# Loops of six edge tiles instead of five, and the zeroing of two DRAM buffers and a broadcast load moved behind the blocks of 32 destinations

## The reference

```python
xn = _layernorm(x)
x = x + gnn(xn @ W, edges) + linear_attention(xn)    # gnn: relu(sum over edges of edge_weight * (xn @ W)[src])
x = x + moe_block(_layernorm(x))                     # attention, gate, one of 8 experts per node
xn = _layernorm(x)
x = x + graph_attention_2_layers(xn, edges) + linear_attention_2(xn)
x = x + ffn_top2(_layernorm(x))
```

## Time and profile before

| | us |
|---|---|
| median of 3 runs | 1269.78 (1269.62 to 1273.46) |
| the profiled execution's own time | 1271.01 |
| its span | 1269.5 |
| PE busy | 1103.7 (87%) |
| DVE busy | 540.2 (43%) |
| ACT busy | 356.5 (28%) |
| POOL busy | 105.8 (8%) |

### The profile page before, as it was taken

How to read it: one execution, slowest core, us unless ns; L and a number is a source line. 1 busy time by engine, 2 the same in 40 slices (tenths; PEclk the granted TensorE clock), 3 DMA queues, 4 the chain that set the end, 5 groups by cost and what they waited for, 6 DMA issues and landing times.

```text
span 1269.5 us, 20489 instructions
## 1 busy us (share of the span) xinstructions
PE 1103.7 (87%) x7358; PEld 747.2 (59%) x7359; DVE 540.2 (43%) x1451; ACT 356.5 (28%) x901; POOL 105.8 (8%) x170
## 2 busy tenths in 40 slices
PE   4477899889999837999998579998979998997898
PEld 2367754647777433555554257786557777573763
DVE  7577773344446411111111145543325545368350
ACT  1001230014555221222222135443115555011230
POOL 5112300000000050000000230000000000000000
PEclk9799999989999957999999889999989999998799
DMA  7500014100000258910499470000121000000001
GB/s 219 130 1 2 2 64 169 58 1 25 26 26 2 83 209 298 396 48 17 178 405 400 176 278 26 26 1 1 67 74 43 26 10 2 34 1 1 1 8 33
DMA packets 19105, 113.09 MB, mean 89 GB/s; under 512 B 4906, under 2 KB 6433, under 8 KB 14948
## 3 DMA queue, kind: packets, MB, share of 16 engines
q1 hardware_dynamic: 13406, 100.95, 21.1%
q0 software_dynamic: 5632, 11.23, 3.3%
HBM read 103.04 MB, written 9.11 MB: 88 GB/s over the span
## 4 chain that ended last, share of the span: by engine, by line
PE 75%; DVE 10%; DMA 6%; issue 4%; ACT 3%; DVEq 1%; POOL 1%; SPq 0%; POOLq 0%; ACTq 0%
PE psum L543 10%; PE psum L694 9%; PE psum L844 7%; PE psum L825 7%; PE psum L717 5%; PE psum L555 5%; PE psum L748 5%; PE psum L699 5%; PE psum L604 4%; PE psum L730 4%; PE psum L903 3%; PE psum L925 3%; DMA arena<-in_moe_b 2%; DVE arena L1214 2%; PE psum L782 1%
## 5 line engine op out<-in xcount | busy, mean ns | idle before, releaser
L543 PE MATMUL psum<-arena 128*125 128x512 f32 x320 | 142.7, 606 | 1.8 <-ACT arena L938 1.4
L998 ACT ACTIVATE arena<-arena,small 125x625 f32<-125x625 f32 x120 | 97.0, 809 | 90.5 <-DVE small L1340 90.5
L694 PE MATMUL psum<-arena 128*128 128x313 f32 (+1 forms) x384 | 112.5, 444 | 8.4 <-DMA arena<-in_att 7.1
L543 PEld LDWEIGHTS psum<-arena 128*125 128x125 f32 x320 | 61.0, 192 | 80.4 <-issue 75.3
L825 PE MATMUL psum<-arena 128*64 128x512 f32 x448 | 100.2, 600 | 6.5 <-DMA arena<-in_moeW 5.1
L844 PE MATMUL psum<-arena 128*64 128x256 f32 x896 | 99.8, 381 | 3.5 <-DMA arena<-in_moe_b 3.5
L1056 ACT ACTIVATE arena<-psum,cols 128x64 f32<-128x64 f32 x224 | 47.3, 361 | 195.9 <-PE psum L831 195.9
L694 PEld LDWEIGHTS psum<-arena 128*128 128x128 f32 x384 | 72.4, 195 | 38.0 <-issue 9.7
L604 PE MATMUL psum<-arena 125*128 x1150 | 74.2, 223 | 23.1 <-DVE arena L1214 23.1
L1214 DVE TENSOR_SCALAR arena<-arena 125x628 bf16<-125x628 f16 x230 | 77.0, 399 | 35.3 <-PE psum L604 20.3
L1340 DVE CUSTOM_DVE_ANT_0 arena<-psum,cnt_adj 125x625 f32<-125x625 f32 x80 | 61.5, 806 | 71.6 <-PE psum L717 71.6
(11 more groups left out here) (246 smaller groups left out, 1321.8 us busy)
## 6 DMA issues: line engine op xcount, KB each, us to landing
arena<-in_moeW SPq DMA_DIRECT2D x16, 4096.0 KB, 17.9
arena<-in_att SPq DMA_DIRECT2D x36, 256.0 KB, 2.8
arena<-in_l1W SPq DMA_DIRECT2D x2, 2048.0 KB, 15.8
token_rows<-arena POOLq DMA_DIRECT2D x19, 128.0 KB, 13.1
rows<-in_rows SPq DMA_DIRECT2D x1, 2240.0 KB
expert_rows<-arena POOLq DMA_DIRECT2D x17, 128.0 KB, 13.0
arena<-token_rows POOLq DMA_DIRECT2D x16, 128.0 KB, 7.8
arena<-in_gnnWo SPq DMA_DIRECT2D x2, 1024.0 KB, 6.1
```

Source lines behind the costliest of these rows:

```text
L543: mm = pe.matmul(bank(b, NP, D), srcT[:, k, c * NP:(c + 1) * NP], ring[n % 2][:, k, :], start=(k == 0), stop=(k == KC - 1))
L694: mm = pe.matmul(bank(b, P, width), aw[:, w, k, :], srcT[:, k, o:o + width], start=(k == 0), stop=(k == KC - 1))
L998: act.activation(Sx[u % 3][h], Sx[u % 3][h], ACT.Exp, bias=small[0:NP, 80 + n:81 + n], scale=-1.0, accum_out=small[0:NP, 120 + n:121 + n]) ...
```

## The change

`GT` is 6: six tiles a turn, six buffers, and one more padded tile (`TP` 165 instead of 164). The turns of the 20 windows, counted on the inputs, go from 8, 4, 3, 3, 2, 2, 2, 2, 2, 2, 2, 2, 2, 2, 2, 1, 2, 1, 1, 1 (46 turns, 230 tiles) to 7, 3, 3, 2, 2, 2, 2, 2, 2, 2, 1, 1, 1, 1, 1, 1, 1, 1, 1, 1 (37 turns, 222 tiles).

SP sends `rows` only when all windows are done. POOL zeroes the DRAM buffers after the last window's sums. The zeroed piece of SBUF that this reads lies elsewhere, so ACT waits for the zeroing before it writes there (T3, in stage moT).

```diff
-GT = 5
+GT = 6
...
-        zero_rows_sb = at(o_D + TP * 2 * DW, TT, D)
+        zero_rows_sb = at(o_T + 2 * KC * N + 2 * NC * 3 * DW, TT, D)
...
             sp.dma_start(cols[:], ins["cols"]).then_inc(ld_const, 16)
-            for p in SPLIT:
-                sp.dma_start(rows[p], ins["rows"].partition_broadcast(p.stop - p.start)).then_inc(ld_const, 16)
             sp.dma_start(gate_b[:], ins["gate_b"].partition_broadcast(NP)).then_inc(ld_const, 16)
...
+            sp.wait_ge(win_full, NW)
+            for p in SPLIT:
+                sp.dma_start(rows[p], ins["rows"].partition_broadcast(p.stop - p.start)).then_inc(ld_const, 16)
...
-            pool.wait_ge(ld_ring[0], 16)
-            pool.wait_ge(consts, 14)
-            for t in range(MAXT + 2):
-
-                pool.dma_start(xs_dram[t * TT:(t + 1) * TT, :], zero_rows_sb).then_inc(
-                    zero_rows if t <= MAXT else M["st"], 16)
-                if t < MAXT:
-                    pool.dma_start(ys_dram[t * TT:(t + 1) * TT, :], zero_rows_sb).then_inc(zero_rows, 16)
...
             pool.memset(bd[:, :, :], 0.0).then_inc(bd_zero, 1)
+            pool.wait_ge(consts, 14)
+            for t in range(MAXT + 2):
+
+                pool.dma_start(xs_dram[t * TT:(t + 1) * TT, :], zero_rows_sb).then_inc(
+                    zero_rows if t <= MAXT else M["st"], 16)
+                if t < MAXT:
+                    pool.dma_start(ys_dram[t * TT:(t + 1) * TT, :], zero_rows_sb).then_inc(zero_rows, 16)
...
             feature_exps(range(8, 8 + NC))
+            act.wait_ge(zero_rows, 16 * (2 * MAXT + 1))
+            act.wait_ge(M["st"], 16)
             cols_out("moT", T3)
```

More of the change, by code:

```diff
@@ L189, in build @@
         parts = [at(o_T + 2 * KC * N + i * NC * 3 * DW, NP, NC, 3 * DW) for i in range(2)]
-        assert o_D + TP * 2 * DW + D <= AR
         assert oa[0] <= o_cnt
```

## The result

The changed kernel takes 1255.2 us (median of 4 runs, 1252.92 to 1260.38) against 1270.38 us for the kernel before (4 runs, 1269.62 to 1273.46) on the same chip: ratio 0.9875, 95% interval 0.9848 to 0.9901. The nearest case was the rival "loads freed", 1257.2. The profiled execution is the longest of the four: span 1258.8, own time 1260.38, where before it was 1269.5 and 1271.0. So the two traces hold 10.7 us of the 15.2 us between the medians. The other 4.5 lie between runs of one and the same kernel, and no trace shows them.

What follows compares the result with a forecast made beforehand. The prediction took PE, busy for 87% of the span, as the bound. Turns -7.8, padding +0.1, loads 0, constants +5.6 and clock +1.0 gave -1.1 us from the median 1269.8: 1268.7 us, range 1256 to 1273.

Steps and rivals of the forecast that it cites:

- loads freed: Rival: DMA traffic slowed the register loads, so the windows start 11.5 us earlier; 1257.2 us, chance 0.35.
- Part 1: Window loops: nine turns fewer save 19.3 us, the added tiles cost up to 11.5; gain 7.8 us taken, bounds 7.8 to 11.2.
- the sixth tile: Tile added to each of the 37 turns: 0.31 us each on PE, 11.5 us in all, or down to 0.22, 8.1 us.
- free tiles: Rival: the window loops' added tile hides in PE's idle time, 37 x 0.22; 1265.3 us, lower edge of the forecast's 0.52.
- Part 2: Register loads ahead of the windows: DMA silence leaves them long, gain 0; bounds no gain to 11.5 us earlier.
- Part 3: Row constants sent at the windows' end (W) land at W + 10.8, making mq's last unit 5.6 us late; bounds 4.3 and 9.8.
- the landing beyond W + 13: Sign against the forecast: mq's first unit coming later than 13 us after the windows' end (W).
- the start before 54: Sign against the forecast: PE's first window matmul before 54 us, meaning the register loads felt the traffic.
- windows under 88: Sign against the forecast: windows shorter than 88 us, meaning the added tile hides.
- Part 4: PE's clock may fall while it idles ahead of agg, ending agg later: 1.0 us taken, bounds 0 and 1.8.
- Part 5: Late zeroing, done 30 to 34 us after the windows' end, stays hidden by 0 to 4 us behind the mask; no cost.
- The sum: Whole kernel: turns -7.8, padding +0.1, loads 0, constants +5.6, clock +1.0, together -1.1 us.

Runs made afterwards that it cites:

- turns_alone: Changed kernel with both transfers (row constants and zeroing) back in their early places, loops of six kept: 1247.94 us, ratio 0.9823.
- turns_unaligned: Six tiles a turn, both transfers early, and the loaded numbers two words further on, at word 4998, off a multiple of four: 1260.29 us, ratio 0.9919.
- loads_by_place: Separate kernel computing nothing of the reference: PE loads 20 registers from many SBUF places, quiet, beside zeroing, beside weight loads; 1.36 to 4.93 us a load when quiet.
- five_late: Changed kernel with five tiles a turn instead of six, so `bounds` at word 4678, both transfers late: 1268.94 us, ratio 1.0008.
- aligned_alone: Kernel before with two words left empty, so `bounds` starts at word 4680, a multiple of four, instead of 4678: 1257.37 us, ratio 0.9903.
- rows_early: Changed kernel with the row constants sent early again, zeroing still late: 1247.1 us, ratio 0.9823.
- changed_again: Changed kernel, no edit, measured and profiled once more: 1254.29 us, ratio 0.9874.
- zero_early: Changed kernel with the zeroing back in its early place, row constants still late: 1259.56 us, ratio 0.9901.
- zeroed_piece_moved: Kernel before with only the SBUF piece that the zeroing reads (and ACT's wait) moved to its place in the changed kernel: 1267.46 us, ratio 0.9975.
- rows_after_first_window: Changed kernel with the row constants sent when the first window, not the last, has filled: 1246.06 us, ratio 0.9794.

## Why the prediction was wrong

**Part 1, turns: right in kind, too small.** 37 turns came, and the windows took 87.8 us where 90.6 were predicted: -10.4, inside the bounds of 7.8 to 11.2. The mis-sized term is the sixth tile. I charged PE's 0.31 us. From the two lengths, the 37 added tiles cost 19.3 - 10.4 = 8.9 us, 0.24 each. That is close to my rival "free tiles" (0.22), but not for its reason: the sixth tile doesn't hide in PE's idle time, for the wait on DVE ahead of a turn is 0.50 us in both kernels (23.1 us in 46 turns, 18.4 in 37). A turn's matmuls run 1.57 us for five tiles and 1.83 to 1.85 for six in the timelines, so one tile more costs PE itself 0.26 to 0.28; 0.31 was the mean of five, with what the group costs once in it. The windows are as long in turns_alone and turns_unaligned, with all transfers early.

**Part 2, the start: the step that failed.** "I take the long loads as they are: gain 0." The gain was 11.9 us (13.3 like with like). I had argued from the loads of one register, 298 to 327 ns even in a stretch of 545 GB/s, that traffic doesn't slow a load. That was the wrong witness, twice. The 545 GB/s are a mean over 2 us: from 693.5 to 694.5, around the load at 693.9, the trace has no packet at all. And the traffic of that stretch is weights coming in from DRAM, which slows no load (4.76, 1.36 and 0.30 us beside it in loads_by_place, the last of them amid packets); what ran at the start was the zeroing, out of SBUF, and that does. A share of busy DMA engines doesn't say what kind of transfer it is.

The second half was in neither my forecast nor my rival: the price of a bulk load depends on where its first number lies, 1.4 or 4.8 us quiet, 5.6 or 18.9 beside the zeroing. The diff moves `bounds` by 318 words without naming it. So the rival "loads freed" came near in time, with half the reason: its bound was 46.0 for the first window matmul, by 0.30 us a register; the loads then took 0.08 a register, and PE's stage ahead, which ended at 43.44, set the start at 45.67. Its mechanism was real: traffic slowed the loads, and quiet alone gave 9.7 to 11.0 us of the start (five_late). But it wasn't needed: the place alone gave 10.7 (aligned_alone), and with the place right the late zeroing brings the start from 46.03 to 44.24 and no time that could be told (turns_alone and rows_early, both 0.9823). The two gains overlap; they don't add. That the whole came out at the rival's 1257.2 is luck in part: a larger gain at the start and in the windows met a larger loss behind them.

The Trainium skill's rule of about 200 ns a register ("Runtime: NRT & Kernel Launch", section "Instruction fetch mechanics"), which I had set against the trace, agrees with one of the four cases here: 20 unaligned registers, quiet, 4.74 to 4.93 us, 0.24 each. Aligned they cost 0.07. The Trainium skill has that section's load and store prices for registers that the runtime loads; here the numbers lie in SBUF, and the measurement decides. The rule gave the right doubt, that something slowed the load. The start of 44.2 that I had worked out by it, held by `hot_dst`, is where changed_again and rows_early have it (44.24), but with a load of 1.55 us and not of 4: DVE's builder sets it.

**Part 3, the constants: the right mechanism, +7.9 for +5.6.** The eight units took 13.3 us (146.88 to 160.16), as worked out (13.4). The mis-sized term is the landing, W + 13.4 for W + 10.8. I had taken 323 GB/s from the queue's rate with other loads, 7.9 us, and 1.5 us besides; with the engines for itself (zero_early) this broadcast had its packets in 10 us and released DVE 3 us after the last. My reason for the long end of the bounds, the zeroing beside it, was wrong: there was none in zero_early. With the landing beyond W + 13, a sign that I had named as "wrong" came, as did two others, the start before 54 and windows under 88; and by my own sum, -1.1 + 2.6 = +1.5, the kernel would have been no faster, had the rest come as forecast. five_late, without the turns, shows how a quiet start and this loss cancel.

**Part 4, the clock: +2.1 for +1.0,** a little over its upper bound of 1.8. It fell before agg, as feared: 0.50 from 154.1 to 167.7, and agg 23.90 us against 21.69 where it didn't fall. The transposes in between, on which I had counted, did not keep it up: from the end of mq's matmuls, 150.56, to 154.1 they were 0.99 us of work. All four traces with late constants have the half clock at agg's start (agg 23.20 to 23.95 us); of the nine with early ones eight have not (21.69 to 21.70), but zeroed_piece_moved has (0.50 up to 180, agg 23.37). So the late constants bring the fall on; it can come without them.

**Part 5, the zeroing: right.** SP passes its wait for the zeroing, then waits for the mask:

```profile
SPq L358 <- DMA token_rows<-arena: 29.8, 1, 29.8
SPq L359 <- DVE cnt_adj L1234: 5.7, 1, 5.7
```

(engine and line, waited for: us in total, times, longest.) The mask comes last, by 5.7 us where I had 0 to 4: the zeroing is done at W + 30.7, as worked out, and the mask is later, at W + 36.5 for W + 34.2.

**The sum** with what was measured: -11.9 - 10.4 + 7.9 + 2.1 = -12.3, for -1.1 predicted. The error is 11.2 us; the start alone is 11.9, and the other terms nearly cancel.

**What stays open.** Why a load from an unaligned place costs 3.5 times as much. Loads that fetch four numbers at once from a place on a multiple of four, and one by one elsewhere, would take five or twenty times the 0.30 us of one number, 1.5 or 6.1; that is near the 1.36, less near the 4.75, and no run shows the fetches. Nor is it shown what it is in the zeroing that slows a load (no other transfer that reads SBUF was run beside one), nor what the 3 us after the last packet of the constants are. And the runs of one kernel lie up to 15 us apart (the kernel before, 1263.40 to 1278.42 in 19 runs); the granted clock in the late stages varies with them, and what sets it wasn't looked for.

## What to carry to other kernels

Where loads of registers stand on the path, let the numbers begin on a multiple of four words, and keep transfers like the zeroing away from them: here that was 17.4 against 1.6 us, and either of the two alone brought most of the gain at the start. A size that changes moves all that is laid out behind it, so compare the addresses of what sequencers read, not only the instructions. A transfer put "where the engines are free" belongs there only if its reader comes late enough: the constants cost 10 us behind the last window and nothing that can be told behind the first. rows_after_first_window, with 1246.06 us (0.9794), differs from the changed kernel in that single number, and the two intervals don't meet.

## What the runs showed of the hardware

- A load of 20 registers takes 1.36 us from a multiple of four words, 4.74 to 4.93 from elsewhere; beside DRAM zeroing from SBUF (194 GB/s) 5.45 to 5.74 and 18.87. One register: 0.30 and 1.17.
- Beside 446 GB/s from DRAM into SBUF the same loads take 1.36, 4.76 and 0.30.
- The broadcast of 20 KB of rows into 125 partitions, 2.56 MB, releases its reader after 13.0 us (zero_early): 10 us of packets, 256 GB/s, and 3 us with the engines still. That it shares them with the zeroing didn't lengthen it: 12.81 us in the changed kernel.
- In the changed kernel mq's matmuls ended at 150.56 and PE's granted clock fell to 0.50 at 154.1, after 0.99 us of transposes in the 3.5 us between. It was back at 1.00 at 167.7, with PE at work without a gap since 163.3.
